# A ring of gathers: one landing wait for each group of four in place of one for each gather

## What is computed

```python
def _gcn_conv(x, W, b, src, dst, norm, n_nodes):
    h = x @ W
    msg = h[src] * norm[:, None]
    out = jax.ops.segment_sum(msg, dst, num_segments=n_nodes)
    return out + b
...
att = jnp.einsum('ehd,ehd->eh', q[dst], k[src]) / scale
...
alpha = ex / (s[dst] + 1e-16)
msg = (v[src] * alpha[:, :, None]).reshape(-1, D)
aggr = jax.ops.segment_sum(msg, dst, num_segments=n)
x = x + (aggr @ Wo[l] + bo[l])
```

## Time and profile before

| | us |
|---|---|
| median of 3 runs | 7751.77 |
| lowest and highest | 7746.49, 7763.63 |
| the profiled execution, its own time | 7761.23 |
| its span, first to last instruction | 7759.4 |
| GpSimd gathers, pass 0 | 819 to 1653 |
| pass 1 | 1689 to 2597 |
| pass 2 | 2637 to 3551 |
| pass 3 | 3593 to 4409 |
| pass 4 | 4443 to 6002 |
| pass 5 | 6102 to 7660 |

### The profile page before, as it was taken

One profiled execution on the slowest core, in us unless ns is written; L12 is line 12 of the kernel. 1 busy time (PEld: TensorE's weight loads), 2 busy tenths in 40 slices (PEclk: granted clock), 3 DMA queues, 4 the chain that ended last, 5 costly groups with the idle time before them and its releaser, 6 DMA issues.

```text
span 7759.4 us, 116895 instructions
## 1 busy us (share of the span) xinstructions
PE 5133.9 (66%) x25317; PEld 3898.4 (50%) x25540; DVE 3876.6 (50%) x10619; ACT 677.3 (9%) x1598; POOL 3351.6 (43%) x3512
## 2 busy tenths in 40 slices
PE   2677556765788667886566555666777655666666
PEld 1122455654566556665445444455666444555555
DVE  8544355652333323343334445556666545566665
ACT  0011000000000000000000100011112100111111
POOL 0000455545444454443555454455554254545542
PEclk9955666777899878997677677788888777888887
DMA  1011322332333333333222233333333233333331
GB/s 43 33 50 66 104 77 77 99 90 76 108 121 112 95 89 100 103 99 101 74 78 80 73 101 100 99 101 104 104 103 99 66 103 98 101 101 104 101 95 55
DMA packets 308017, 695.49 MB, mean 90 GB/s; under 512 B 68843, under 2 KB 118116, under 8 KB 306526
## 3 DMA queue, kind: packets, MB, share of 16 engines
q0 software_dynamic: 146944, 381.90, 17.5%
q10 hardware_dynamic: 94612, 196.31, 7.4%
q1 hardware_dynamic: 66250, 114.82, 5.0%
HBM read 624.93 MB, written 67.83 MB: 89 GB/s over the span
## 4 chain that ended last, share of the span: by engine, by line
DMA 33%; issue 25%; PE 18%; POOL 9%; DVE 9%; DVEq 3%; ACT 1%; POOLq 1%; SPq 0%; ACTq 0%
DMA ring<-rows,idx_stage 32%; POOL ring L1391 9%; PE acc_ps L1835 5%; PE acc_ps L1853 2%; PE acc_ps L1787 1%; PE q_ps L1777 1%; PE acc_ps L1747 1%; PE q_ps L1747 1%; DVE even_rows L582 1%; PE acc_ps L1748 1%; PE bank L1889 1%; PE q_ps L1748 1%; DVE masks L808 1%; DVE dots L993 1%; PE bank L2028 1%
## 5 line engine op out<-in xcount | busy, mean ns | idle before, releaser
L1391 POOL DMA_INDIRECT ring<-rows,idx_stage x3360 | 3312.1, 986 | 3247.2 <-DMA ring<-rows,idx_stage 1846.4
L1853 PE MATMUL acc_ps<-ring,masks 128*128 x4800 | 1226.3, 419 | 954.5 <-SPq L1304 587.7
L1853 PEld LDWEIGHTS acc_ps<-ring,masks 128*128 128x128 f32 x4800 | 975.2, 253 | 1171.6 <-issue 1082.7
L1777 PE MATMUL q_ps<-odd_rows,conv_only 128*128 (+1 forms) x3904 | 766.6, 365 | 951.3 <-DVE conv_only L796 871.5
L788 DVE SCALAR_TENSOR_TENSOR masks<-dst_f,neg_first,lane 128x256 f32<-128x256 f32 x1200 | 548.7, 483 | 1334.9 <-PE acc_ps L1853 1012.0
L1777 PEld LDWEIGHTS q_ps<-odd_rows,conv_only 128*128 128x128 f32 x3904 | 675.7, 264 | 1026.5 <-issue 1022.5
L1787 PE MATMUL acc_ps<-msg,masks 128*128 x3904 | 644.9, 316 | 156.7 <-DVE msg L1005 142.0
L1787 PEld LDWEIGHTS acc_ps<-msg,masks 128*128 128x128 f32 x3904 | 601.3, 224 | 279.0 <-issue 267.3
L796 DVE TENSOR_SCALAR conv_only<-conv_only,node_id 128x512 f32 x488 | 240.5, 493 | 727.2 <-SPq L1333 553.6
L1376 POOL COPY idx_stage<-src_idx 128x28 int32 (+1 forms) x126 | 33.3, 265 | 1060.4 <-DVE turn_b L729 810.4
L808 DVE SCALAR_TENSOR_TENSOR masks<-dst_f,neg_first,lane 128x512 f32<-128x512 f32 x488 | 366.9, 752 | 236.6 <-PE acc_ps L1787 197.9
(11 more groups left out here) (278 smaller groups left out, 6240.6 us busy)
## 6 DMA issues: line engine op xcount, KB each, us to landing
conv_only<-dst_rows SPq DMA_DIRECT2D x394, 256.0 KB
ring<-rows,idx_stage POOLq DMA_INDIRECT x3360
adjacency<-odd_rows ACTq DMA_DIRECT2D x10, 3136.0 KB, 8.9
conv_only<-adjacency ACTq DMA_DIRECT2D x70, 384.0 KB
msg<-adjacency ACTq DMA_DIRECT2D x60, 384.0 KB
wide<-adjacency ACTq DMA_DIRECT2D x60, 384.0 KB
turn_b<-adjacency ACTq DMA_DIRECT2D x60, 384.0 KB
part<-adjacency ACTq DMA_DIRECT2D x30, 448.0 KB
```

Of the source, the lines that this page charges most:

```text
L1391: pool.indirect_dma_start(ring[:, j, 0:WIDTH[p]], None, tables[p][:, :], bass.IndirectOffsetOnAxis(ap=idx_stage[:, half, j:j + 1], axis=0) ...
L1777: ins = pe.matmul(to, mask_t[:, u, j, :], q_rows[:, bass.ds(t + u, 1), :].rearrange("p a f -> p (a f)"), start=u == 0, stop=u == nxt)
L1853: ins = pe.matmul(to, masks[:, u, j, :], rhs, start=False, stop=final and j == GC - 1)
```

## The change

The wait on `landed[j - 2]` leaves the loop over a group's slots. In its place stands one wait ahead of the group, for q > 0, on `landed[q * GC - 2]`: the third gather of the preceding group. The wait for room comes behind it. The first group of a lap waits for no landing at all.

```diff
                         pool.wait_ge(idx_staged, staged + 1)
                         pool.sem_inc(staging_seen, 1)
 
+                    if q > 0:
+                        pool.wait_ge(landed[q * GC - 2], lap * 16 + 16)
+                        pool.sem_inc(slots_seen, 1)
                     pool.wait_ge(groups_freed, lap * RG + q + 1)
                     pool.sem_inc(slots_seen, 1)
                     for j in range(q * GC, (q + 1) * GC):
-                        if j >= 2:
-                            pool.wait_ge(landed[j - 2], lap * 16 + 16)
-                            pool.sem_inc(slots_seen, 1)
                         pool.indirect_dma_start(
```

## The result

The changed kernel takes 7124.2 us in the median of 4 runs (7115.5 to 7140.7), the kernel before 7757.2 in 4. The recorded ratio is 0.9189, with a 95% interval of 0.9178 to 0.9200 (the two medians themselves give 0.918): 633 us less, where 450 were forecast. The profiled execution took 7115.5 us, with a span of 7112.9. It is faster for the reason given, but the time lies under the bottom of the range (7170), so the prediction was wrong in size.

What follows compares the result with a forecast made beforehand. Bound by a chain of waits through gathers that move little, nothing being full. Gains of 252 (attention), 100 (fourth convolution) and 98 us (first three) sum to 450, giving 7311, or 7302 for a median; range 7170 to 7545 us.

Steps and rivals of the forecast that it cites:

- A group's new time: Four gathers with one landing wait: 6.57 us, 6.37 in a lap's mean in attention; 6.11 in the fourth convolution.
- The wait for room at no cost: First gather's room wait, now behind its landing wait, costs nothing; a tenth more hop in 720 groups would add 58 us.
- First stretch of an attention pass: First 557 us, 71 groups from 7.85 to 6.37 us each: a gain of 105 us a pass.
- Middle stretch: Next 560 us of an attention pass: 63.6 us of DVE's waiting to take from, a third taken, 21 us.
- the last third: Last 442 us of an attention pass: no waits for gathers there, so no gain and an unchanged length.
- Fourth convolution: Gathers could give 132 us, with 233.8 us of PE's waiting to take from; three quarters taken, 100 us.
- First three convolutions: At most 353.9 us of PE's waiting; only waits between dense pairs go, 28% taken, 98 us.
- Compute takes over at once: Outside attention's first stretches DVE and PE are late next, so only 210 us is kept: 7542 us; chance 0.08.
- The landing grows: With three gathers under way each lands later; some 50 us would be left: 7702 us; chance 0.05.
- Slower by queueing: Gathers, adjacency parts and row broadcasts queue on the same 16 DMA engines: about 8047 us; chance 0.04.
- Slower by the instruction: Unbroken gathers held to 1.7 us each, a group costing 8.0 us without landing waits: about 7894 us; chance 0.03.

Runs made afterwards that it cites:

- c3: The changed kernel with its two waits ahead of a group in the other order, freed slots first, then the third landing; 7088.0 us (0.912).
- g1: The kernel before with two matmuls of zeros behind each gathered group of convolution passes 2 and 3; 7777.5 us against 7776.6 (1.000).
- h1: The changed kernel run again unedited; 7332.2 us against 7777.3 for the kernel before (0.942).
- d4: c3 with the landing wait moved from the third to the second gather of the preceding group; 6798.6 us (0.876).
- e3: The changed kernel with no landing wait on GpSimd at all, only the room in the ring holding it; 8019.0 us (1.031).
- d1: The changed kernel run again unedited; 7137.1 us against 7765.2 for the kernel before (0.920).

## Why the prediction was right in kind and wrong in size

The sum by its terms, from the two profiled executions:

- *A group's new time.* Forecast 6.57 us with a landing wait and 6.37 in the mean of a lap, early in attention. Measured 465.5 us for 284 gathers in the windows below, 6.56 a group. That is a mean, so it stands against the 6.37 and is 0.19 us over it; that it looks like the 6.57 is chance. Forecast 4.0 us from third to next, measured 3.98 in the median and 4.20 in the mean. In the fourth convolution the median is 3.53 us where 3.7 was forecast. Right in the main.
- *The wait for room at no cost.* The step "I cost this at nothing" was wrong: c3 prices it at 45 us. It is inside the 58 that the text gave to the range, and it goes the other way than the miss.
- *First stretch of an attention pass.* Forecast 105 us, measured 558 - 465.5 = 92.5, from the start of the first gather to that of the 285th. Right within 0.2 us a group.
- *Middle stretch.* Here the step "I take a third, 21 us" failed. Windows of the first attention pass after, by the same gathers as the earlier trace rows:

```profile
4089.00:4554.50 465.50, 279.45 (x284) 0.83 0.41 121
4554.50:5020.00 465.50, 280.92 (x282) 0.90 0.41 121
5020.00:5482.00 462.00, 213.37 (x219) 0.88 0.34 99
```

  The middle went from some 560 to 465.5 us, and the last third, which was to keep its length, grew from 442 to 462. Net that is 74 us where I took 21. DVE's wait for SP in the middle is now 4.3 us in all, of 63.6: nearly all of it could be had, in patches or not, and the 74 us are even more than the 63.6 that I took for the most. Over both passes the attention gave 306 us for 252.
- *Fourth convolution.* Forecast 100, measured 113. Right.
- *First three convolutions.* The step "I take 28%, 98 us" failed; they gave 247, and the 149 us between are three quarters of the excess. I capped them by PE's waits at one line and then took a small part, reasoning that the ring fills during dense pairs. Those waits fell by 175 us in these passes, from 338.0 to 163.1, so they do not even hold the gain. GpSimd's own waits say it better. In the second pass before:

```profile
POOL ring L1391 <- DMA ring<-rows,idx_stage: 269.6, 189, 4.2
POOL ring L1391 <- issue: 132.1, 240, 3.1
POOL ring L1391 <- DVEq L838: 66.5, 15, 15.7
```

  and after:

```profile
POOL ring L1391 <- DMA ring<-rows,idx_stage: 136.4, 77, 3.9
POOL ring L1391 <- issue: 111.6, 351, 1.6
POOL ring L1391 <- DVEq L838: 105.1, 12, 25.6
```

  GpSimd waited for room on DVE in only 66.5 of its 908 us, dense pairs included, and for landings in 269.6. The first two rows fell by 154 us together, the third gave back 39, near the pass's 103. I had quoted the longest wait for room, 19.6 us, and not the sum of that row in this pass.
- *A term that was missing.* PE's busy time fell by 35 us in this pass (677.26 to 642.45), with the clock from 0.87 to 0.93. The sum has no such term. From PE's side these 35 us, and the 80 by which its waits for landed groups fell (133.3 to 53.0 us), less 10 us more of waiting for DVE's masks, come to 105, near the pass's 103. g1 found no gain from the clock alone, so I hold the clock for a consequence of shorter waits; that is argued, not shown.

By size: +54 for attention, +13 for the fourth, +149 for the first three, less some 20 between the passes: 196 of the 196.5 us between 450 and the spans' 646.5.

**Chance of the kind.** In the second kind the same kernel gains 445 us, next to the forecast's 450. That is no credit to the sum: there the first three convolutions gave more than 98 too (799, 807 and 844 us long in h1) and the late attention lost. From the third stretch of an attention pass on, h1 takes 505 us for what the changed kernel does in 462.

**The rivals.** *Compute takes over at once* did not happen: the middle stretch and three convolutions kept most of their gain. *The landing grows* did not: third to next is 3.98 us in the median, and from issue to landing it is 2.8 in the changed kernel and 2.8 in d4. *Slower by queueing*: the DMA share rose to 0.41 and d4's to 0.50, and the landings stayed as long. But the second kind, with e3 at 1.03 of before, shows that more in flight can lose. In h1 third to next is 4.02 us in the median, as in the result, and what is late are PE's semaphores; for e3, whose trace has no landing times, that it is the same is argued from its chain (18% "another core or an unknown queue", DMA 1%). *Slower by the instruction* did not happen either: between 938 and 1990 ns, and 991 in the mean against 986 before:

```profile
L1391 POOL DMA_INDIRECT ring<-rows,idx_stage x3360: 938/946/1990, 818.2 to 7007.3; - x198
```

**The skill's rules.** The mean of 991 ns and the 1.25 us between unbroken gathers say that DVE seldom holds GpSimd here. The Trainium skill, "SBUF — State Buffer", section "SBUF: two separate sides", has GpSimd blocked from writing descriptors while DVE is in a two-port mode; the trace allows for at most a rare hold. The landing took 2.8 us in the median, and 3.01 and 3.35 in the chains shown. The Trainium skill, "DMA: Bandwidth & Descriptors", section "Anatomy of one DMA", gives by my estimate 2.3 us, and with it a time some 150 us lower, near the result. The agreement is by accident: the group came at 6.56 us, later and not earlier than the sum had it, and the excess lay elsewhere.

## What to carry to other kernels

Price a supply that is late from the supplier's own side: add up what it waits for (landings and hops against room). The part that isn't room can be had until the consumer's pace is met; here 154 us of it went in one pass, and 39 came back as waits for room. The consumer's wait at one line is neither a cap (175 us of it went where 247 were gained) nor evenly hard to get. When several waits stand before one instruction, put the one that ends last right before it. And repeat a gain of this sort in a second job: the same kernel here gained 8.0 to 8.2% in three jobs and 5.8% in a fourth, and the next step (one landing earlier) is the best of all in one kind of job and a loss in the other, though with its two waits in the other order.

## What the hardware showed that was not expected

In the second kind of run a semaphore that ACT awaits from PE came 2.1 us late, behind matmuls whose records show nothing, and often only in kernels with more than two gathers in flight: 42 late steps of 50 in h1, 11 in d1 and in g1. The changed kernel took 7137 and 7332 us on one chip. The gather instruction is as long in both (988 ns), and what else the profile shows of the two runs gives no cause. A wait that has been met is not free either: between a landing and the gather behind it lie 0.80 us with one increment and 0.95 with a second wait and two increments, and 0.76 us of it is "issue" in both. And the granted clock rose as the waiting fell: 0.87 in the second pass before, 0.93 after, 0.94 in d4.
